# A decoder layer's causal mask: from a TensorE accumulation to GpSimd selects on the exponentials

## The chip, the cores and the metric

The kernel runs on one core of a Trainium2 chip. The metric is the device time of one execution in microseconds. It is float32 work with some bfloat16 matmuls, about 86,000 instructions in one launch.

## The reference

64 sequences of 256 tokens with 256 channels go through self-attention, cross-attention and a routed feed-forward net, each on a layer-normalized input and each added to the residual. The change touches the self-attention only (16 heads of 16 channels):

```python
att = jnp.einsum('bhtd,bhsd->bhts', q, k) / math.sqrt(D)
causal = jnp.tril(jnp.ones((T, T), dtype=bool))
att = jnp.where(causal, att, -jnp.inf)
att = jax.nn.softmax(att, axis=-1)
y = jnp.einsum('bhts,bhsd->bhtd', att, v)
```

Then follow the cross-attention, over 120 context rows with one key found per context row by an argmax, and the feed-forward net (256 to 1024 to 256, one of four experts for each token).

## The kernel before

The first three quarters of the run are a loop over the 64 sequences (`steps`), and the last quarter is a loop over 35 tiles of 512 tokens for the feed-forward net. Five engines run five programs of their own, each a fixed order written out by hand. They meet only in semaphores. The loop is a pipeline: iteration i projects sequence i, attends within sequence i-1, does the first half of the cross-attention of i-2, the second half of i-3 and the routing of i-4. One iteration takes about 49 us.

Queries and keys are split in bfloat16 parts, written to DRAM and read back in packed form (SyncE's queue: `store_parts`, `pack`). `cq_parts` to `parts_qc` to `QC` is that round trip for the cross-attention.

The self-attention computes the scores twice. The first pass (`self_for_max`, row by query) gives each query's maximum, and has a causal mask of its own, `mask_s`. The second pass (`self_scores`, row by key, steps n = 0 to 11) includes the negative maximum in the product. Three steps make a group g of four heads: two steps of two heads each for the first 128 keys against all 256 queries, and one step of four heads for the last 128 keys against the last 128 queries. Each step ends with one more matmul, L647, that adds `mask_t` (-1e30 above the diagonal) through an identity matrix onto the 128x128 blocks on the diagonal: 256 columns in the first two steps of a group, 512 columns in the third. ScalarE then takes the exponential (`self_exp`, L964) into `PA` (first 128 keys) or `PB` (last 128 keys), and `self_values` (L660 for PA, L662 for PB) multiplies with the values. `self_values` of group g waits until exponential 3g+3 is done.

The order on TensorE in the last part of an iteration: scores 0, 1, 2, a small ranking product, score 3; then `cross_for_max` 0 (L724), which needs `QC` from DRAM; then scores and cross products in turn (score 4, cross 1, score 5, cross 2, values of group 0, score 6, cross 3, and so on up to score 11), values of group 1 after cross 5, values of group 2 after score 11, values of group 3, a small transpose, and `turn_y` (L559), which transposes the attention's result. Score n waits for exponential n-2, since there are two PSUM banks for scores. VectorE takes the maxima of the cross products (`cross_max`, L1131), and after the sixth it takes the statistics of the next sequence (`ln1_statistics`, L1092 and L1096).

GpSimd's order in an iteration: `q_parts` and `k_parts` (L1528, L1531), `cq_parts` (L1535), the reciprocal root for the third layer norm, the root for the next sequence's first layer norm (`root`, L1480 and L1483), two indirect DMAs of routed rows (`send_rows`), the root for the second layer norm, and nine small steps that split the context keys (`split_k`). Each engine executes its queue strictly in order.

Of the kernel before, what the change touches and what calls it, by code (L numbers as in the profile page):

```python
# [8 lines left out]
BF16 = mybir.dt.bfloat16  # L9
# [5 lines left out]
P = 128  # L15
C = 256
KC = C // P
T = 256
# [48 lines left out]
def decoder_kernel(nc, x, ctxT, wqkvT, bqkT, bv, wqT, wkvT, wcT, w_router, w1, b1T, wo, bo, gamma, beta, consts, out):  # L67
# [3 lines left out]
    with ExitStack() as stack:  # L71
        def sb(name, shape, dt=F32):
            return stack.enter_context(nc.sbuf_tensor(name, shape, dt))

        def signal(name, per_sequence, step=1):
            return Signal(stack.enter_context(nc.semaphore(name)), per_sequence * step)
# [8 lines left out]
        psum = stack.enter_context(nc.psum_tensor("psum", [P, 8, 512], F32))  # L85
# [12 lines left out]
        ident_bf = sb("ident_bf", [P, P], BF16)  # L98
        ones_bf = sb("ones_bf", [P, P], BF16)
        mask_s = sb("mask_s", [P, P], BF16)  # L100
        mask_t = sb("mask_t", [P, P], BF16)
        consts_sb = sb("consts_sb", [P, TILE_NOS + B * T // TILE + E - 1])
        iota_m = consts_sb[:, 3 * P:3 * P + M]
        part_mask = consts_sb[:, 3 * P + M:3 * P + M + 3]
# [32 lines left out]
        def during_attention(name, shape, dt=F32):  # L137
            return attention_stack.enter_context(nc.sbuf_tensor(name, shape, dt))
# [14 lines left out]
        QP = during_attention("QP", [P, 2, H, T], BF16)  # L153
        KP = during_attention("KP", [P, 2, H, T], BF16)
# [4 lines left out]
        PA = during_attention("PA", [P, H, T])  # L159
        PB = during_attention("PB", [P, H, P])  # L160
# [124 lines left out]
        place_step = signal("place_step", 5)  # L285
        consts_in = semaphore("consts_in")
        consts_ready = semaphore("consts_ready")
        VECTOR_CONSTS = 9
        gpsimd_consts = semaphore("gpsimd_consts")
        GPSIMD_CONSTS = 7  # L290
        N_FIRST_LOADS = 3
# [22 lines left out]
        st_made = signal("st_made", 12)  # L314
# [18 lines left out]
        q_mid = signal("q_mid", 1)  # L333
        k_mid = signal("k_mid", 1)
        exp_done = signal("exp_done", 12)
        mxT_copied = signal("mxT_copied", 1)
        yT_copied = signal("yT_copied", 2)
        czT_copied = signal("czT_copied", 1)
# [41 lines left out]
        passed_pool = semaphore("passed_pool")  # L380
# [14 lines left out]
        def runs(i, lag):  # L395

            return not isinstance(i, int) or 0 <= i - lag < B
# [151 lines left out]
        def _(pe):  # L549
            def latest(*readers):  # L550


                for sig, b, k in readers:
                    if not isinstance(b, int) or 0 <= b < B:
                        return sig.sem, sig.value(b, k)
                return consts_ready, VECTOR_CONSTS

# [65 lines left out]
            def self_scores(i, par, n):  # L623

                b, q = i - 1, 1 - par
                KS = KR + 2
                g, r = divmod(n, 3)
                bank = ST_BANKS[n % 2]
                if n == 0:
                    pe.wait_ge(mx_packed[q].sem, mx_packed[q].value(b // 2))  # L630
                elif n == 1:
                    pe.wait_ge(*latest((cyC_copied, i - 3, 1), (exp_done, i - 2, 12)))
                else:
                    pe.wait_ge(exp_done.sem, exp_done.value(b, n - 1))
                if r < 2:
                    for j in range(2):
                        h = 4 * g + 2 * r + j
                        pe.matmul(psum[:, bank, j * T:(j + 1) * T], KP[0:KS, q, h, 0:P], QP[0:KS, q, h, :], start=(j == 0), stop=False, skip_group_check=True)  # L638
                    diagonal = psum[:, bank, :].rearrange("p (j k) -> p j k", j=2)[:, :, 0:P]
                    masks = 2  # L640
                else:
                    for j in range(4):
                        h = 4 * g + j
                        pe.matmul(psum[:, bank, j * P:(j + 1) * P], KP[0:KS, q, h, P:T], QP[0:KS, q, h, P:T], start=(j == 0), stop=False, skip_group_check=True)  # L644
                    diagonal = psum[:, bank, :]
                    masks = 4
                pe.matmul(diagonal, ident_bf[:], mask_t[:].unsqueeze(1).broadcast_to([P, masks, P]), start=False, stop=True, skip_group_check=True).then_inc(st_made.sem, 1)  # L647

            def self_values(i, par, g):

                b, q = i - 1, 1 - par
                bank, col = Y_BANKS[g // 2], (g % 2) * T
                if g == 0:
                    pe.wait_ge(v_copied.sem, v_copied.value(b))
                    pe.wait_ge(*latest((match_step, i - 2, 2 * NT), (q_rest_made, i, 1)))
                elif g == 2:
                    pe.wait_ge(*latest((kmask_made, i - 2, 1), (k_rest_made, i, 1)))
                pe.wait_ge(exp_done.sem, exp_done.value(b, 3 * g + 3))
                for j in range(4):
                    pe.matmul(psum[32 * j:32 * j + 32, bank, col:col + T], V[:, q, 0, 4 * g + j, :], PA[:, 4 * g + j, :], start=True, stop=False, skip_group_check=True)  # L660
                for j in range(4):
                    last = pe.matmul(psum[32 * j:32 * j + 32, bank, col + P:col + T], V[:, q, 1, 4 * g + j, :], PB[:, 4 * g + j, :], start=False, stop=True, skip_group_check=True)  # L662
                if g % 2 == 1:
                    last.then_inc(pv_made.sem, 1)
# [176 lines left out]

            pe.wait_ge(consts_ready, VECTOR_CONSTS)
            pe.wait_ge(first_weights_in, 16 * N_FIRST_LOADS)
# [226 lines left out]
        def _(dve):  # L1070
            made = [0]

            def constant(ins):
                ins.then_inc(consts_ready, 1)
                made[0] += 1
# [1 line left out]
            dve.wait_ge(consts_in, 16)  # L1077
            constant(dve.tensor_copy(ident_bf[:], consts_sb[:, 0:P]))
            constant(dve.tensor_copy(mask_s[:], consts_sb[:, P:2 * P]))
            constant(dve.tensor_copy(mask_t[:], consts_sb[:, 2 * P:3 * P]))  # L1080
            constant(dve.memset(ones_bf[:], 1.0))
            constant(dve.tensor_copy(before_bf[:], consts_sb[:, BEFORE:BEFORE + P]))
            constant(dve.tensor_copy(next_row[:], consts_sb[:, NEXT_ROW:NEXT_ROW + E]))
# [2 lines left out]
            constant(dve.memset(minus_half[:], -0.5))  # L1086
            assert made[0] == VECTOR_CONSTS

# [234 lines left out]

            dve.wait_ge(consts_ready, VECTOR_CONSTS)
            ln1_statistics(0, 0)
# [149 lines left out]
        def _(pool):  # L1475
            def root(b, step, mean_var, rs, made, eps, NT=NT):

                pool.wait_ge(step.sem, step.value(b, 2 * NT))
                pool.sem_inc(passed_pool, 1)
                pool.tensor_scalar(rs[:], mean_var[:, :, 1], eps, None, ALU.add).then_inc(made.sem, 1)  # L1480
                pool.wait_ge(made.sem, made.value(b, 1))
                pool.sem_inc(passed_pool, 1)
                pool.tensor_tensor(rs[:], rs[:], minus_half[:, 0:NT], ALU.pow).then_inc(made.sem, 1)  # L1483

            def send_rows(i, par):

                b = i - 4
                pool.wait_ge(place_step.sem, place_step.value(b))
                pool.sem_inc(passed_pool, 1)
                pool.wait_ge(x2_made.sem, x2_made.value(b))  # L1490
                pool.sem_inc(passed_pool, 1)
                pool.wait_ge(number_made.sem, number_made.value(b))
                pool.sem_inc(passed_pool, 1)
                for t in range(NT):
                    pool.indirect_dma_start(out=rows_dram, out_offset=bass.IndirectOffsetOnAxis(ap=row_u[:, par, t:t + 1], axis=0),
                                            in_=x2[:, par, t, :], in_offset=None).then_inc(rows_sent[par].sem, 16)
# [27 lines left out]
            def body(i, par):  # L1524
                if runs(i, 0):
                    pool.wait_ge(q_mid.sem, q_mid.value(i))
                    pool.sem_inc(passed_pool, 1)
                    pool.tensor_tensor(q_parts[:, 2, :], q_rest[:], q_parts[:, 1, :], ALU.subtract).then_inc(q_low.sem, 1)  # L1528
                    pool.wait_ge(k_mid.sem, k_mid.value(i))
                    pool.sem_inc(passed_pool, 1)  # L1530
                    pool.tensor_tensor(k_parts[:, 2, :], k_rest[:], k_parts[:, 1, :], ALU.subtract).then_inc(k_low.sem, 1)  # L1531
                if runs(i, 2):
                    pool.wait_ge(cq_mid.sem, cq_mid.value(i - 2))
                    pool.sem_inc(passed_pool, 1)
                    pool.tensor_tensor(cq_parts[:, 2, :], cq_rest[:], cq_parts[:, 1, :], ALU.subtract).then_inc(cq_low.sem, 1)  # L1535
                if runs(i, 3):
                    root(i - 3, ln3_step, rmv, rrstd, ln3_rstd, LN_EPS)
                if runs(i, 0):
                    root(i + 1, ln1_step, mv, rstd, ln1_rstd, LN_EPS)
                if runs(i, 4):  # L1540
                    send_rows(i, par)
                if runs(i, 1):
                    root(i - 1, ln2_step, cmv, crstd, ln2_rstd, LN_EPS)
                    split_k(i, par)

            pool.wait_ge(consts_ready, VECTOR_CONSTS)
            root(0, ln1_step, mv, rstd, ln1_rstd, LN_EPS)
# [136 lines left out]
```

## Time and profile before

| | |
|---|---|
| median of 3 runs | 4378.67 us (4378.36 to 4382.7) |
| profiled execution, span | 4384.2 us |
| TensorE busy | 3487.1 us, 80% |
| VectorE busy | 3030.9 us, 69% |
| ScalarE busy | 1595.7 us, 36% |
| GpSimd busy | 1468.2 us, 33% |
| granted TensorE clock, mean | 0.870 of full |
| loop over sequences | to about 3240 us |

The span runs from the first to the last instruction of the profiled execution; no time of that execution outside its span is given, so the span is compared with the median of the timed runs directly. Busy time is the share of an engine's instructions that are executing, and a high share doesn't show that the engine sets the end.

### The profile page before, as it was taken

What the parts mean: (1) busy time and instruction counts of PE and PEld (TensorE: products, weight loads), DVE (VectorE), ACT (ScalarE), POOL (GpSimd) and SP (SyncE); (2) the same over time, 40 slices, a digit from 0 to 9 for tenths busy, and PEclk for the clock granted to TensorE, in tenths of its full rate; (3) what the DMA queues carried; (4) which work ended last, traced back from release to release, by engine and by line L of the source; (5) the groups of instructions that cost most, each with busy time, mean ns of one, the idle gap of its engine ahead of it and who ended that gap; (6) DMA issues with size and microseconds to landing.
All of it is one profiled execution on the core that took longest, in us unless ns stands there. A gap on an engine that the chain in (4) does not pass through costs nothing.

```text
span 4384.2 us, 86021 instructions
## 1 busy us (share of the span) xinstructions
PE 3487.1 (80%) x26632; PEld 2620.2 (60%) x26632; DVE 3030.9 (69%) x7302; ACT 1595.7 (36%) x2976; POOL 1468.2 (33%) x1785
## 2 busy tenths in 40 slices
PE   5788778887788777887788778887748888888887
PEld 3555555555555555555555555555537777777777
DVE  3666656665666656665666656665649999999997
ACT  2444444444444444444444444444412222222221
POOL 3222222222222222222222222222225656565655
PEclk7888888888888888888888889888858889888888
DMA  6455554455455554555455554555321212212120
GB/s 126 78 92 94 96 89 84 89 99 93 85 90 95 94 89 84 93 96 95 82 90 95 94 89 89 92 95 93 61 76 63 68 65 67 67 64 67 65 67 32
DMA packets 341784, 366.25 MB, mean 84 GB/s; under 512 B 58456, under 2 KB 319071, under 8 KB 341728
## 3 DMA queue, kind: packets, MB, share of 16 engines
q1 hardware_dynamic: 324768, 330.85, 41.8%
q0 software_dynamic: 12864, 33.64, 2.1%
q10 hardware_dynamic: 4096, 1.06, 0.1%
q8 instruction: 30, 0.49, 0.1%
q14 instruction: 26, 0.21, 0.0%
HBM read 251.56 MB, written 113.32 MB: 83 GB/s over the span
## 4 chain that ended last, share of the span: by engine, by line
PE 29%; DVE 24%; DMA 21%; issue 12%; ACT 4%; POOL 4%; SPq 3%; DVEq 1%; POOLq 0%; ACTq 0%
DMA parts_qc<-cq_parts 12%; DMA QC<-parts_qc 8%; DVE hT_high L1405 8%; PE psum L660 4%; PE psum L724 4%; SPq L457 3%; PE psum L565 3%; PE psum L638 3%; PE psum L647 2%; PE psum L611 2%; PE psum L559 2%; PE psum L751 2%; POOL cq_parts L1535 2%; PE psum L662 2%; PE psum L644 2%
## 5 line engine op out<-in xcount | busy, mean ns | idle before, releaser
L1131 DVE TENSOR_REDUCE cnegmax<-psum 128x4 f32<-128x480 f32 x512 | 324.3, 654 | 662.1 <-PE psum L724 661.9
L964 ACT ACTIVATE PA<-psum 128x512 f32<-128x512 f32 x512 | 294.9, 596 | 881.3 <-PE psum L647 879.9
L724 PE MATMUL psum<-KCx,QC 97*128 97x120 bf16 x2048 | 243.7, 256 | 332.7 <-DMA QC<-parts_qc 331.0
L1058 ACT ACTIVATE hT<-psum,b_sb 128x512 f32<-128x512 f32 x280 | 193.2, 690 | 848.1 <-PE psum L884 848.1
L900 PE MATMUL psum<-wo_high,hT_low 128*128 128x256 f32 x1120 | 385.4, 344 | 131.1 <-DVE hT_low L1408 69.0
L1124 DVE TENSOR_REDUCE negmax<-psum 128x2 f32<-128x512 f32 x512 | 340.9, 687 | 154.1 <-PE psum L614 153.8
L724 PEld LDWEIGHTS psum<-KCx,QC 97*128 97x128 bf16 x2048 | 190.4, 119 | 404.3 <-issue 347.3
L638 PE MATMUL psum<-QP,KP 98*128 98x256 bf16 x1024 | 240.8, 327 | 164.7 <-DMA QP<-mxT 164.7
L1405 DVE CAST hT_high<-hT 128x512 fp32r<-128x512 f32 x280 | 359.7, 1295 | 3.9 <-ACT hT L1058 3.7
L900 PEld LDWEIGHTS psum<-wo_high,hT_low 128*128 128x128 f32 x1120 | 252.7, 226 | 177.1 <-DVE hT_low L1408 95.9
L900 PE MATMUL psum<-wo_low,hT_high 128*128 128x256 f32 x1120 | 354.9, 317 | 0.0
L900 PE MATMUL psum<-wo_high,hT_high 128*128 128x256 f32 x1120 | 352.7, 315 | 0.0
L1480 POOL TENSOR_SCALAR rstd<-mv 128x2 f32<-128x2 f32 x65 | 15.2, 234 | 991.4 <-DVE mv L1096 991.4
L976 ACT ACTIVATE PC<-psum 120x512 f32<-120x512 f32 x512 | 291.3, 594 | 86.2 <-PE psum L740 80.2
L647 PE MATMUL psum<-mask_t,ident_bf 128*128 128x256 bf16 (+1 forms) x768 | 292.5, 381 | 0.0
L565 PE MATMUL psum<-zT,wqkv_sb 128*128 128x256 f32 x1024 | 241.0, 389 | 23.6 <-ACT zT L917 23.6
L900 PEld LDWEIGHTS psum<-wo_low,hT_high 128*128 128x128 f32 x1120 | 256.2, 229 | 0.0
L900 PEld LDWEIGHTS psum<-wo_high,hT_high 128*128 128x128 f32 x1120 | 254.1, 227 | 0.0
L614 PE MATMUL psum<-mask_s,ident_bf 128*128 128x256 bf16 (+1 forms) x768 | 240.3, 313 | 0.0
L565 PEld LDWEIGHTS psum<-zT,wqkv_sb 128*128 128x128 f32 x1024 | 191.6, 192 | 62.8 <-issue 32.5
L884 PE MATMUL psum<-fzT_high,w_low 128*128 128x512 f32 x560 | 219.4, 392 | 7.6 <-DVE fzT_low L1400 7.6
L1535 POOL TENSOR_TENSOR cq_parts<-cq_rest,cq_parts 128x512 bf16<-128x512 f32 x64 | 74.0, 1156 | 444.9 <-ACT cq_parts L917 444.9
(211 smaller groups left out, 8867.8 us busy)
## 6 DMA issues: line engine op xcount, KB each, us to landing
QP<-parts_q SPq DMA_DIRECT2D x384, 128.0 KB, 4.5
KP<-parts_k SPq DMA_DIRECT2D x384, 128.0 KB, 7.8
QC<-parts_qc SPq DMA_DIRECT2D x384, 128.0 KB, 4.6
w_sb<-in_w SPq DMA_DIRECT2D x35, 1024.0 KB, 4.8
parts_q<-q_parts SPq DMA_DIRECT2D x64, 384.0 KB, 2.6
parts_k<-k_parts SPq DMA_DIRECT2D x64, 384.0 KB, 2.6
parts_qc<-cq_parts SPq DMA_DIRECT2D x64, 384.0 KB, 8.4
fx<-rows_dram SPq DMA_DIRECT2D x35, 514.0 KB, 3.8
```

What stands on the lines that cost most here:

```text
L565: last = pe.matmul(psum[:, bank, m * width:(m + 1) * width], lhs(kc, m), rhs(kc), start=(kc == 0), stop=(kc == KC - 1))
L614: pe.matmul(diagonal, ident_bf[:], mask_s[:].unsqueeze(1).broadcast_to([P, masks, P]), start=False, stop=True, skip_group_check=True).then ...
L638: pe.matmul(psum[:, bank, j * T:(j + 1) * T], KP[0:KS, q, h, 0:P], QP[0:KS, q, h, :], start=(j == 0), stop=False, skip_group_check=True)
L647: pe.matmul(diagonal, ident_bf[:], mask_t[:].unsqueeze(1).broadcast_to([P, masks, P]), start=False, stop=True, skip_group_check=True).then ...
L724: last = pe.matmul(psum[:, bank, j * M:(j + 1) * M], QC[0:KS, par, 4 * g + j, t * P:(t + 1) * P], KCx[0:KS, par, 0:M], start=True, stop=True)
L884: last = pe.matmul(psum[:, bank, :], lhs, rhs, start=(n == 0), stop=(n == len(products) - 1))
L900: last = pe.matmul(psum[:, 4 + half, j * C:(j + 1) * C], lhs, rhs, start=(m == 0 and n == 0), stop=(m == MI - 1 and n == 2))
L964: act.activation(dst, psum[:, ST_BANKS[n % 2], :], ACT.Exp, scale=D ** -0.5).then_inc(exp_done.sem, 1)
L976: act.activation(PC[0:M, 2 * n:2 * n + 2, :].rearrange("p h n -> p (h n)"), psum[0:M, ST_BANKS[n % 2], :], ACT.Exp, scale=D ** -0.5).then_ ...
L1124: dve.tensor_reduce(negmax[:, 1, h:h + 2], bank.rearrange("p (h k) -> p h k", h=2), AX_X, ALU.max).then_inc(max_done.sem, 1)
L1131: dve.tensor_reduce(cnegmax[:, t, 4 * g:4 * g + 4], psum[:, S_BANKS[n % 2], 0:4 * M].rearrange("p (h k) -> p h k", h=4), AX_X, ALU.max).th ...
L1405: dve.tensor_copy(hT_high[:, m, :], hT[:, m, :]).then_inc(h_high_made.sem, 1)
```

## The change

The mask matmul of the second score pass goes away, with the constant `mask_t`, and the last score matmul of a step signals `st_made` in its place. GpSimd, for each group of four heads, waits for the group's third exponential and then runs two affine selects in place: one on the first 128 columns of `PA` of the four heads, one on `PB` of the four heads, each 128 partitions by 4 x 128 float32. Weights of keys later than the query become 0. `self_values` waits for the second of these selects, not for the exponential. On GpSimd, groups 0 to 2 stand after the root of the third layer norm and before the root of the next sequence's first layer norm; group 3 stands after that root and before `send_rows`. The first pass keeps its `mask_s`.

```diff
-                pe.matmul(diagonal, ident_bf[:], mask_t[:].unsqueeze(1).broadcast_to([P, masks, P]), start=False, stop=True, skip_group_check=True).then_inc(st_made.sem, 1)
+                last.then_inc(st_made.sem, 1)
...
-                pe.wait_ge(exp_done.sem, exp_done.value(b, 3 * g + 3))
+                pe.wait_ge(causal.sem, causal.value(b, 2 * g + 2))
...
-            constant(dve.tensor_copy(mask_t[:], consts_sb[:, 2 * P:3 * P]))
...
+            def drop_later_keys(b, g):
+
+                heads = slice(4 * g, 4 * g + 4)
+                pool.wait_ge(exp_done.sem, exp_done.value(b, 3 * g + 3))
+                pool.sem_inc(passed_pool, 1)
+                pool.affine_select(out=PA[:, heads, 0:P], in_=PA[:, heads, 0:P], pattern=[[0, 4], [1, P]], base=0, channel_multiplier=-1,
+                                   compare_op=ALU.is_ge, fill=0.0).then_inc(causal.sem, 1)
+                pool.affine_select(out=PB[:, heads, :], in_=PB[:, heads, :], pattern=[[0, 4], [1, P]], base=0, channel_multiplier=-1,
+                                   compare_op=ALU.is_ge, fill=0.0).then_inc(causal.sem, 1)
...
                 if runs(i, 3):
                     root(i - 3, ln3_step, rmv, rrstd, ln3_rstd, LN_EPS)
+                if runs(i, 1):
+                    for g in range(3):
+                        drop_later_keys(i - 1, g)
                 if runs(i, 0):
                     root(i + 1, ln1_step, mv, rstd, ln1_rstd, LN_EPS)
+                if runs(i, 1):
+                    drop_later_keys(i - 1, 3)
                 if runs(i, 4):
                     send_rows(i, par)
```

## Rows read from the trace of the kernel before

**Rows 1.** The first page: its span, and busy time of each engine.

```profile
span 4384.2 us, 86021 instructions
...
PE 3487.1 (80%) x26632; PEld 2620.2 (60%) x26632; DVE 3030.9 (69%) x7302; ACT 1595.7 (36%) x2976; POOL 1468.2 (33%) x1785
```

**Rows 2.** The page: the chain that ended last, by engine, then by line.

```profile
PE 29%; DVE 24%; DMA 21%; issue 12%; ACT 4%; POOL 4%; SPq 3%; DVEq 1%; POOLq 0%; ACTq 0%
DMA parts_qc<-cq_parts 12%; DMA QC<-parts_qc 8%; DVE hT_high L1405 8%; PE psum L660 4%; PE psum L724 4%; SPq L457 3%; PE psum L565 3%; PE psum L638 3%; PE psum L647 2%; PE psum L611 2%; PE psum L559 2%; PE psum L751 2%; POOL cq_parts L1535 
```

**Rows 3.** Waits from 400 to 3100 us: waiter, releaser: us in total, times, longest.

```profile
PE psum L724 <- DMA QC<-parts_qc: 291.0, 55, 6.2
```

**Rows 4.** TensorE in order of time: start us, us, engine, line, out<-in [idle before].

```profile
1886.52 0.56 PE L724 MATMUL psum<-KCx,QC 97*128 97x120 bf16 x4 [5.87 <-DMA QC<-parts_qc]
...
1887.29 0.42 PE L647 MATMUL psum<-mask_t,ident_bf 128*128 128x256 bf16 x1
1887.51 0.61 PE L724 MATMUL psum<-KCx,QC 97*128 97x120 bf16 x4
...
1891.11 0.27 PE L647 MATMUL psum<-mask_t,ident_bf 128*128 128x256 bf16 x1
1891.22 0.37 PE L724 MATMUL psum<-KCx,QC 97*128 97x120 bf16 x4
...
1892.83 0.64 PE L660 MATMUL psum<-PA,V 128*32 128x256 f32 x8
...
1895.05 0.38 PE L647 MATMUL psum<-mask_t,ident_bf 128*128 128x512 bf16 x1
1895.36 0.64 PE L660 MATMUL psum<-PA,V 128*32 128x256 f32 x8
...
1896.12 0.64 PE L660 MATMUL psum<-PA,V 128*32 128x256 f32 x8
...
1897.69 1.09 PE L559 MATMUL psum<-consts_sb,yT 128*128 128x128 f32 x8 [0.42 <-ACT yT L917]
```

**Rows 5.** The page's costliest groups: line, engine, operation | busy, mean ns | idle before.

```profile
L647 PE MATMUL psum<-mask_t,ident_bf 128*128 128x256 bf16 (+1 forms) x768 | 292.5, 381 | 0.0
```

**Rows 6.** GpSimd groups by shape over the whole run.

```profile
L1528 POOL TENSOR_TENSOR q_parts<-q_rest,q_parts 128x512 bf16<-128x512 f32 x64 | 73.8, 1153 | 12.2 <-ACT q_parts L917 9.5
...
L1510 POOL TENSOR_SCALAR kc_b<-kc_m,consts_sb 96x120 f32<-96x120 bf16 x64 | 37.1, 580 | 13.3 <-POOL kc_a L1509 13.3
...
L1549 POOL MEMSET V<- 128x2048 f32 x1 | 1.8, 1797 | 0.0
```

**Rows 7.** GpSimd in order of time, in the same iteration.

```profile
1895.54 0.24 POOL L1480 TENSOR_SCALAR rstd<-mv 128x2 f32<-128x2 f32 x1 [15.11 <-DVE mv L1096]
1895.96 0.71 POOL L1483 TENSOR_TENSOR rstd<-rstd,minus_half 128x2 f32<-128x2 f32 x1 [0.18 <-POOL rstd L1480]
```

**Rows 8.** ScalarE in order of time: the last exponentials of groups 0 to 3.

```profile
1880.23 0.60 ACT L964 ACTIVATE PB<-psum 128x512 f32<-128x512 f32 x1 [0.22 <-PE psum L647]
...
1889.01 0.60 ACT L964 ACTIVATE PB<-psum 128x512 f32<-128x512 f32 x1 [0.66 <-PE psum L647]
...
1892.73 0.60 ACT L964 ACTIVATE PB<-psum 128x512 f32<-128x512 f32 x1 [0.16 <-PE psum L647]
...
1895.46 0.60 ACT L964 ACTIVATE PB<-psum 128x512 f32<-128x512 f32 x1 [0.16 <-PE psum L647]
```

**Rows 9.** VectorE in order of time, in the same iteration.

```profile
1894.92 0.42 DVE L1096 BATCH_NORM_AGGREGATE mv<-stats 128x2 f32<-128x6 f32 x2
```

**Rows 10.** Busy us by engine in stretches; PEclk, DMA share, GB/s stand last.

```profile
1876.30:1880.80 4.50, 2.02 (x21) 1.16 (x19) 2.48 (x10) 1.65 (x4) 0.94 (x2) 1.00 0.58 138
...
1886.50:1891.10 4.60, 4.58 (x38) 3.03 (x39) 2.57 (x5) 1.19 (x2) 0.00 (x0) 0.50 0.00 0
...
1896.70:1900.00 3.30, 2.54 (x31) 1.87 (x20) 2.39 (x10) 1.60 (x4) 2.19 (x2) 1.00 0.14 45
```

**Rows 11.** The same view for a stretch of the iteration before.

```profile
1836.90:1843.30 6.40, 6.32 (x51) 4.49 (x52) 3.37 (x8) 1.99 (x4) 0.00 (x0) 0.50 0.00 0
```

More of the change, by code:

```diff
@@ L100, in decoder_kernel @@
         mask_s = sb("mask_s", [P, P], BF16)
-        mask_t = sb("mask_t", [P, P], BF16)
         consts_sb = sb("consts_sb", [P, TILE_NOS + B * T // TILE + E - 1])
@@ L287, in decoder_kernel @@
         consts_ready = semaphore("consts_ready")
-        VECTOR_CONSTS = 9
+        VECTOR_CONSTS = 8
         gpsimd_consts = semaphore("gpsimd_consts")
@@ L335, in decoder_kernel @@
         exp_done = signal("exp_done", 12)
+        causal = signal("causal", 8)
         mxT_copied = signal("mxT_copied", 1)
@@ L637, in self_scores @@
                         h = 4 * g + 2 * r + j
-                        pe.matmul(psum[:, bank, j * T:(j + 1) * T], KP[0:KS, q, h, 0:P], QP[0:KS, q, h, :], start=(j == 0), stop=False, skip_group_check=True)
-                    diagonal = psum[:, bank, :].rearrange("p (j k) -> p j k", j=2)[:, :, 0:P]
-                    masks = 2
+                        last = pe.matmul(psum[:, bank, j * T:(j + 1) * T], KP[0:KS, q, h, 0:P], QP[0:KS, q, h, :], start=(j == 0), stop=(j == 1), skip_group_check=True)
                 else:
@@ L643, in self_scores @@
                         h = 4 * g + j
-                        pe.matmul(psum[:, bank, j * P:(j + 1) * P], KP[0:KS, q, h, P:T], QP[0:KS, q, h, P:T], start=(j == 0), stop=False, skip_group_check=True)
-                    diagonal = psum[:, bank, :]
-                    masks = 4
-                pe.matmul(diagonal, ident_bf[:], mask_t[:].unsqueeze(1).broadcast_to([P, masks, P]), start=False, stop=True, skip_group_check=True).then_inc(st_made.sem, 1)
+                        last = pe.matmul(psum[:, bank, j * P:(j + 1) * P], KP[0:KS, q, h, P:T], QP[0:KS, q, h, P:T], start=(j == 0), stop=(j == 3), skip_group_check=True)
+                last.then_inc(st_made.sem, 1)
             def self_values(i, par, g):
```

## The prediction

> **What bounds the kernel now.** I read the first page, then the chain, the waits, and one iteration engine by engine. The page shows TensorE at 80% and GpSimd at 33% busy [rows 1], which invites the thought that work should go from the one to the other. The chain corrects it: TensorE is only 29% of the chain that ended last, VectorE 24%, and DMA 21%, most of it the round trip of `cq_parts` through DRAM [rows 2]. The waits say where that trip is felt: TensorE stands before cross product 0 for 291.0 us in 55 iterations, 5.3 us in each [rows 3]. So an iteration is a loop of three parts: a head (from `turn_y` to `cq_parts`), the round trip, and a tail that starts when `QC` has landed and ends with the values of group 3. What TensorE does before cross product 0 is hidden behind the round trip. What it does in the tail is not.
>
> The tail of the iteration that I follow runs from 1886.52 to `turn_y` at 1897.69 [rows 4]. Values of group 1 start at 1892.83, of group 2 at 1895.36, of group 3 at 1896.12, and `turn_y` comes 1.57 us after the last. The next head's first steps wait for that.
>
> **What the change removes.** 768 mask matmuls, 292.5 us busy [rows 5]. Of the twelve in an iteration, four (scores 0 to 3) stand ahead of the wait for `QC` and are worth nothing. The cover is the 5.87 us idle before cross product 0 [rows 4]; they are under 1 us. Eight stand in the tail. What one costs is the distance to the next start, since matmuls overlap: 0.22 us (1887.29 to 1887.51) for 256 columns at the half clock, 0.11 us (1891.11 to 1891.22) at the full one [rows 4], and I count twice that for 512 columns. Scores 4 and 5 run at the half clock (0.22 + 0.43), scores 6 to 11 at the full one (4 x 0.11 + 2 x 0.22): 1.53 us in a tail, if TensorE sets its pace. The dropped copy of `mask_t` on VectorE is one instruction in the setup, hidden behind the first loads, and under 1 us even if it weren't.
>
> **What it adds.** Eight affine selects of 128 x 512 float32 in each iteration, 512 in all. No such instruction is in the trace, so their time S is bounded. The shortest GpSimd work of this kind is a memset, 1797 ns for 2048 elements, so 0.45 us for 512. The nearest in shape is a tensor-tensor of 128x512, 1153 ns [rows 6]. The most expensive slope is that of a tensor-scalar, 580 ns for 120 elements [rows 6] against 0.24 us for 2 [rows 7]: 2.9 ns an element, 0.24 + 510 x 0.0029 = 1.73 us. I take 1.15 us, the row of the same shape, as an estimate: a select reads one operand and not two, but computes an index and a comparison as well. The range keeps 0.45 and 1.73.
>
> The Trainium skill (GPSIMD Engine Reference, section 7) gives 2.03 cycles an element for a body that compares and selects, and half that when unrolled; at its 1.2 GHz that would be 0.87 or 0.44 us for 512 elements. By the first, an S of some 1.0 us with a fixed part, the sum below would be about 4 x 0.15 = 0.6 us an iteration smaller. No row here shows a select. The same page (section 4.1) advises against elementwise work on this engine; that speaks against the change only where GpSimd's time is seen, so the question is where.
>
> **Where the selects stand on the path.** Group 0: its last exponential ends at 1880.83 [rows 8], and GpSimd has been idle since 15.11 us before 1895.54, that is since 1880.43 [rows 7]. Its two selects (2.3 us) end near 1883.3, before `QC` lands at 1886.5: hidden. If the cover were gone, they would cost 2.3 us.
>
> Group 1: the last exponential ends at 1889.61 now [rows 8], about 0.65 us sooner without the masks of scores 4 and 5: 1888.96. GpSimd reacts after about 0.2 us (VectorE's `mv` ends at 1895.34 [rows 9], the root starts at 1895.54 [rows 7]). Selects from 1889.15 to 1891.45. The values of group 1 would come at 1892.83 - 1.09 = 1891.74 (five masks less): just hidden, up to S = 1.25.
>
> Group 2: the exponential ends at 1893.33, less 1.09 is 1892.24; selects 1892.45 to 1894.75. The values of group 2 would come at about 1894.05: a wait of 0.8 us.
>
> Group 3: its select is queued behind the root of the next sequence's first layer norm, and this root is behind group 2's selects. The root needs `mv`, which ends at 1895.34 [rows 9], about 1.1 us sooner now, so it starts when the selects of group 2 let it, 1894.75. It takes 1.13 us (1895.54 to 1896.67 [rows 7]): until 1895.9. The last exponential ends at 1896.06 - 1.53 = 1894.53, long before. Two selects until 1898.2, values of group 3 at 1898.3, where they were at 1896.12 [rows 4]. **The first term is +2.2 us an iteration**, the saved 1.53 us already in it. Written out, the values of group 3 start at the latest of three times: 1893.68 + 4S (group 2's exponential, four selects, the root, 0.1 to TensorE), 1890.37 + 6S (six selects from group 1 on), and 1895.68 + 2S (the root alone ahead, `mv` at 1894.25). At 1.15 the first decides.
>
> Nothing takes that delay up. The ScalarE copy, `turn_y`, the residual and the next head hang on these values, the round trip hangs on the head, and the next iteration waits for `QC` again. The next exponentials wait for the same values (`pv_made`), but come much later. Behind group 3's selects on GpSimd stand `send_rows`, the second layer norm's root and the split of context keys; the root's input comes later by the same delay, and the two indirect DMAs in front of it end before it is due. SyncE's queue gets nothing new. Busy time of GpSimd grows by 512 x 1.15 = 590 us, which by itself costs nothing.
>
> **The clock.** Between the start of group 2's values and that of group 3's, TensorE would now be busy for 0.76 us in some 3.5 to 4.2 us. The stretch before 1880.80 had 2.02 us busy in 4.5, and the clock was granted at half (1.2 GHz) from there on; the one from 1896.70 to 1900.00 had 2.54 in 3.3 and kept full (2.4 GHz) [rows 10]. The new stretch looks like the first. Once low, the clock stayed so for 4.6 us of nearly unbroken work in this tail [rows 10] and 6.4 us in the one before [rows 11]. Such a stretch loses half of itself, 2.3 to 3.2 us, of work that would fall on `turn_y`, the turns and the projections at the head's start. I take 2.6 us as the **second term**; a part could hide behind VectorE's residual and layer norm, and if the clock were low in the whole tail it would be more.
>
> The Trainium skill (TensorE: Matmul & The Clock Gate, section "Why this matters for your kernels") warns of idle gaps between bursts of matmuls that are longer than the gap of some 2.7 us expected here; by it the clock would hold. The trace doesn't bear that out: its stretch of 4.5 us with 2.02 us of work was followed by the half clock. So I follow the trace, and keep the other outcome as the second rival.
>
> **The sum.** 2.2 + 2.6 = 4.8 us in each of the 62 iterations that have all parts (the first and last have less): +298 us. Against the span of 4384.2 that is 4682. The span lies 5.5 us above the median of the timed runs, 4378.67, so the forecast is 4677, said as 4680.
>
> **The rivals.**
> Slower selects. At S = 1.73 the first two times above are 1900.60 and 1900.75, so +4.6, with the clock +7.2 an iteration: +446, 4825. If S were twice the tensor-tensor's, 2.3, six selects decide: 1904.2, +8.1 + 2.6, 4384 + 663, about 5040. For it: the tensor-scalar's slope. Against it: one operand. 15%.
> The clock holds. +2.2 x 62 = +136: 4515. For it: a stretch with 2.54 us of work in 3.3 kept the clock [rows 10], and the new one is the emptier only if both waits come. The Trainium skill's rule on gaps (above) speaks for it too. Against it: the drop in [rows 10]. 15%.
> Short selects. At S = 0.45 the third time decides, 1896.58: +0.46; with the clock's 2.6 +190 (4569), without +29 (4408). 11%.
> Faster. The root is no longer in front: if the statistics come early enough for the root to end before group 3's exponential, the values of group 3 start at 1894.53 + 0.2 + 2S + 0.1. With S = 0.45 that is 1895.73, 0.4 us sooner than before, -25 us: 4355. It decides below S = 0.65, and only with the root gone. As the queue is, the third time above asks for S under 0.22. Against it: the memset's row, and `mv`, whose input is cross maximum 5. 3%.
> No measurable change: S near 0.6 in that same case. 2%.
>
> **How the numbers follow.** The forecast, with S from 0.8 to 1.5 and a lower clock, has 54%; its own range is 2.6 + (1.3 to 3.6) in an iteration, so 4620 to 4765. The range for all reaches down to short selects with a held clock and up past the tensor-scalar's price: 4420 to 4860, which leaves out some 2 in 10, at the top mostly. About 0.2% (9 us) is what a measurement of this kernel can tell from no change. Faster 3%, same 2%, slower 95%.
>
> **What the profile after would show.** The group of the select, with its mean: the largest unknown. L647 gone, TensorE's busy time down by some 290 us minus what a lower clock adds. A wait of L660 for GpSimd's PB, two in an iteration, the longer one 2 to 3 us, none for groups 0 and 1. The root at L1483 directly before group 3's selects. Granted clock falling between 1 and 4 us before group 3's values, and the mean clock under 0.870. The idle time before L724 about as before, since both ends of the round trip shift together; if it shrinks instead, the delay was taken up there, and the prediction is wrong. It is wrong too if selects are under 0.5 us or above 2 us.

## The result, and the profile after

The changed kernel takes 4494.98 us (median of 4 runs, 4487.36 to 4499.14), the kernel before 4378.51 us beside it. The ratio is 1.0253, 95% interval 1.0234 to 1.0271: 2.5% slower, some 111 us, or 1.79 us in each of 62 iterations. The forecast was slower by 6.9%. Its range held the time, its number did not come near.

The first page after: the span, the busy times, and two of the costliest groups, the select on PA and the product of the values.

```profile
span 4497.4 us, 85514 instructions
...
PE 3451.9 (77%) x25864; PEld 2604.6 (58%) x25864; DVE 3081.7 (69%) x7301; ACT 1582.6 (35%) x2976; POOL 1771.7 (39%) x2297
...
L1485 POOL TENSOR_SCALAR_AFFINE_SELECT PA<-PA 128x512 f32<-128x512 f32 x256 | 162.5, 635 | 654.5 <-ACT PB L960 654.0
...
L656 PE MATMUL psum<-PA,V 128*32 128x256 f32 x2048 | 207.2, 484 | 123.4 <-POOL PB L1487 123.4
```

GpSimd's selects take 635 ns each, not 1.15 us. L656 (L660 before) now has idle time in front of it, 123.4 us, all of it ended by GpSimd's second select; the rows of L660 before have none [rows 4]. GpSimd's busy time grew by 303.5 us, and TensorE's fell by only 35 us though 292.5 us of mask matmuls are gone [rows 5].

One tail on TensorE after (start us, us), to set beside [rows 4]: cross product 0, the values of groups 1, 2 and 3, `turn_y`, and the next projections.

```profile
1902.28 0.56 PE L720 MATMUL psum<-KCx,QC 97*128 97x120 bf16 x4 [6.37 <-DMA QC<-parts_qc]
...
1907.64 0.64 PE L656 MATMUL psum<-PA,V 128*32 128x256 f32 x8
...
1909.84 0.64 PE L656 MATMUL psum<-PA,V 128*32 128x256 f32 x8
...
1912.71 0.89 PE L656 MATMUL psum<-PA,V 128*32 128x256 f32 x8 [2.01 <-POOL PB L1487]
...
1914.72 1.87 PE L559 MATMUL psum<-consts_sb,yT 128*128 128x128 f32 x8 [0.52 <-ACT yT L913]
...
1917.80 3.72 PE L565 MATMUL psum<-zT,wqkv_sb 128*128 128x256 f32 x16 [0.33 <-ACT zT L913]
```

ScalarE's last exponentials of groups 1 to 3 in that tail, to set beside [rows 8]:

```profile
1904.13 0.60 ACT L960 ACTIVATE PB<-psum 128x512 f32<-128x512 f32 x1 [0.23 <-PE psum L642]
...
1907.48 0.60 ACT L960 ACTIVATE PB<-psum 128x512 f32<-128x512 f32 x1
...
1909.94 0.60 ACT L960 ACTIVATE PB<-psum 128x512 f32<-128x512 f32 x1
```

VectorE's statistics for the next sequence, to set beside [rows 9]:

```profile
1909.71 0.42 DVE L1091 BATCH_NORM_AGGREGATE mv<-stats 128x2 f32<-128x6 f32 x2
```

And GpSimd's queue in that tail, to set beside [rows 7]: two selects for group 1, two for group 2, the root of the next layer norm, two for group 3.

```profile
1904.89 0.63 POOL L1485 TENSOR_SCALAR_AFFINE_SELECT PA<-PA 128x512 f32<-128x512 f32 x1 [7.43 <-ACT PB L960]
1905.47 0.63 POOL L1487 TENSOR_SCALAR_AFFINE_SELECT PB<-PB 128x512 f32<-128x512 f32 x1
1908.24 0.64 POOL L1485 TENSOR_SCALAR_AFFINE_SELECT PA<-PA 128x512 f32<-128x512 f32 x1 [2.13 <-ACT PB L960]
1908.83 0.63 POOL L1487 TENSOR_SCALAR_AFFINE_SELECT PB<-PB 128x512 f32<-128x512 f32 x1
1910.33 0.23 POOL L1475 TENSOR_SCALAR rstd<-mv 128x2 f32<-128x2 f32 x1 [0.86 <-DVE mv L1091]
1910.75 0.71 POOL L1478 TENSOR_TENSOR rstd<-rstd,minus_half 128x2 f32<-128x2 f32 x1 [0.18 <-POOL rstd L1475]
1911.43 0.63 POOL L1485 TENSOR_SCALAR_AFFINE_SELECT PA<-PA 128x512 f32<-128x512 f32 x1
1912.02 0.63 POOL L1487 TENSOR_SCALAR_AFFINE_SELECT PB<-PB 128x512 f32<-128x512 f32 x1
```

Group 1 starts its selects at 1904.89 and has them at 1906.1; its values start at 1907.64, so they don't wait. Group 2 starts at 1908.24 and has them at 1909.46; its values start at 1909.84 and don't wait either. Group 3's last exponential ends at 1910.54, but GpSimd is in the root from 1910.33 to 1911.46. The root waited 0.86 us for VectorE's statistics, which end at 1910.13. The selects end at 1912.65 and the values of group 3 start at 1912.71, after 2.01 us without work. That is 10.43 us after cross product 0, where it was 9.60 [rows 4].

The rest comes behind it. `turn_y` lasts 1.87 us for 1.09 [rows 4]. The busy time in two stretches shows why (TensorE first, the granted clock third from the end):

```profile
1908.40:1912.00 3.60, 2.30 (x36) 1.32 (x32) 3.46 (x10) 2.17 (x4) 2.55 (x5) 1.00 0.00 0
1912.00:1915.50 3.50, 2.27 (x22) 1.64 (x23) 1.15 (x3) 0.85 (x2) 2.73 (x4) 0.64 0.10 38
```

TensorE was busy for 2.30 us of 3.60 and then ran at 0.64 of the full clock in the next stretch, a mixture of the half and the full level. Shorter stretches part the two:

```profile
1913.00:1916.30 3.30, 2.78 (x26) 2.23 (x19) 0.54 (x3) 0.85 (x2) 1.91 (x2) 0.50 0.23 82
1916.40:1920.00 3.60, 3.27 (x20) 2.81 (x19) 2.56 (x9) 1.15 (x3) 0.48 (x2) 1.00 0.50 157
```

The clock stands at half while `turn_y` runs and is full again before the projections. It doesn't fall in every iteration: `turn_y` takes more than 1.3 us in 55 of the 64 iterations after and in none before. In the iterations after that keep 1.09 us, the two distances behind the values of group 3 are those of the kernel before (1.57 and 2.27 us on the mean, against 1.58 and 2.29).

VectorE's busy time grew too, by 51 us [rows 1]. Two operations that run beside group 3's selects have some 45 us of it. The two before, then after:

```profile
1896.73 0.19 DVE L1111 SCALAR_TENSOR_TENSOR cmx<-cnegmax,cmx 128x32 bf16<-128x32 f32 x1
1896.85 0.73 DVE L1102 TENSOR_SCALAR z<-x_in,mv,rstd 128x256 f32<-128x256 f32 x2
...
1911.53 0.58 DVE L1106 SCALAR_TENSOR_TENSOR cmx<-cnegmax,cmx 128x32 bf16<-128x32 f32 x1
1912.03 1.12 DVE L1097 TENSOR_SCALAR z<-x_in,mv,rstd 128x256 f32<-128x256 f32 x2
```

They end at 1912.11 and 1913.15, and TensorE turns their results after the values of group 3 and after `turn_y`. So this isn't on the path here.

For a whole view I read the same five starts of TensorE in 54 or 55 iterations of every trace and averaged the distances between them. The last column is the period. The kernels of the experiments, described below, stand in it already.

```
us, mean over iterations      cross 0 to       values 3    turn_y to     projections   period
                              values of 3      to turn_y   projections   to cross 0
before                          9.75            1.58         2.29          35.66       49.28
after                          10.59            1.96         3.16          35.37       51.07
masks removed, no select        8.61            1.58         2.29          35.95       48.43
selects added, masks kept      11.21            1.70         2.48          35.79       51.18
group 3 before the root        10.14            1.58         2.56          35.66       49.94
busy wait                      10.79            1.58         2.29          35.88       50.53
group 3 by mask                 8.94            1.58         2.29          35.69       48.50
two more in group 3            12.01            2.01         3.44          35.18       52.64
two more in group 1            10.70            1.78         3.26          35.16       50.89
```

The difference of the periods, 51.07 - 49.28 = 1.79 us, times 62 is 111 us, the whole result. It has three parts: +0.84 up to the values of group 3, +0.38 + 0.87 = +1.25 from there to the projections, and -0.29 in the rest.

### The profile page after: what moved, and what is told of

The parts are those of the page before. It is cut to its first block, busy times and chain, and to the rows that moved or that the text cites. A ratio compares the mean times of both kernels' runs of the same rounds, so it can differ in the third digit from the quotient of the medians.

```text
span 4497.4 us, 85514 instructions
## 1 busy us (share of the span) xinstructions
PE 3451.9 (77%) x25864; PEld 2604.6 (58%) x25864; DVE 3081.7 (69%) x7301; ACT 1582.6 (35%) x2976; POOL 1771.7 (39%) x2297
## 4 chain that ended last, share of the span: by engine, by line
PE 30%; DVE 22%; DMA 20%; issue 13%; ACT 6%; POOL 5%; SPq 3%; DVEq 1%; POOLq 0%; ACTq 0%
DMA parts_qc<-cq_parts 11%; DMA QC<-parts_qc 8%; DVE hT_high L1400 8%; PE psum L565 7%; PE psum L559 4%; SPq L457 3%; PE psum L656 3%; PE psum L720 2%; PE psum L611 2%; PE psum L747 2%; PE psum L896 2%; POOL cq_parts L1540 2%; PE psum L614 1%; ACT PC L972 1%; PE psum L736 1%
## 5 line engine op out<-in xcount | busy, mean ns | idle before, releaser
L720 PEld LDWEIGHTS psum<-KCx,QC 97*128 97x128 bf16 x2048 | 178.0, 120 | 440.4 <-issue 364.2
L1485 POOL TENSOR_SCALAR_AFFINE_SELECT PA<-PA 128x512 f32<-128x512 f32 x256 | 162.5, 635 | 654.5 <-ACT PB L960 654.0
L638 PE MATMUL psum<-QP,KP 98*128 98x256 bf16 x1024 | 226.2, 320 | 144.1 <-DMA QP<-mxT 143.8
L656 PE MATMUL psum<-PA,V 128*32 128x256 f32 x2048 | 207.2, 484 | 123.4 <-POOL PB L1487 123.4
L1475 POOL TENSOR_SCALAR rrstd<-rmv 128x2 f32<-128x2 f32 x64 | 14.2, 222 | 610.1 <-DVE rmv L1091 610.1
```

Source lines behind the costliest of these rows:

```text
L638: last = pe.matmul(psum[:, bank, j * T:(j + 1) * T], KP[0:KS, q, h, 0:P], QP[0:KS, q, h, :], start=(j == 0), stop=(j == 1), skip_group_che ...
L720: last = pe.matmul(psum[:, bank, j * M:(j + 1) * M], QC[0:KS, par, 4 * g + j, t * P:(t + 1) * P], KCx[0:KS, par, 0:M], start=True, stop=True)
```

## The experiments

All were timed beside the kernel before on the same chip. The ratios are to the kernel before and are to be read beside 1.0253 for the change; a ratio times 4378.5 us puts a time on the scale of the expectations.

**1. The removal alone.** The changed kernel without its selects, so keys later than the query keep their weight in the diagonal blocks.

```diff
-                pe.wait_ge(causal.sem, causal.value(b, 2 * g + 2))
+                pe.wait_ge(exp_done.sem, exp_done.value(b, 3 * g + 3))
...
-                    for g in range(3):
-                        drop_later_keys(i - 1, g)
...
-                    drop_later_keys(i - 1, 3)
```

> The mask matmuls of the second score pass are gone and nothing takes their place, so later keys keep their weight within the diagonal blocks. In the changed kernel the values of group 2 start 7.56 us after cross product 0, before it was 8.84, so theory A (TensorE sets the pace of the tail) expects the values of group 3 to start 1.3 to 1.5 us sooner than before in each of 62 iterations: 4379 - 80 to 95, so 4285 to 4300. Rival B (the exponentials or the maxima set the pace of the tail) expects under 0.3 us an iteration, so 4360 to 4380.

Measured: 4320.72 us, ratio 0.9844 (0.9827 to 0.9861), that is -68 us, or 4310 us where 4285 to 4300 was expected. The values of group 3 come 9.75 - 8.61 = 1.14 us sooner, a little under the 1.3 expected. In the table 0.29 us of it is lost between the projections and cross product 0, but the execution in the trace was the slowest of the five (4336.23 us, 15.5 us over the median, 0.25 us an iteration), so that loss may be of this execution alone. Theory A holds in kind: TensorE sets the pace of the tail, and the masks there are worth 1.14 us and not the 1.53 of their summed distances.

**2. The addition alone.** The masks stay, the selects are added as in the change.

```diff
                 pe.matmul(diagonal, ident_bf[:], mask_t[:]...).then_inc(st_made.sem, 1)
...
-                pe.wait_ge(exp_done.sem, exp_done.value(b, 3 * g + 3))
+                pe.wait_ge(causal.sem, causal.value(b, 2 * g + 2))
...
+                    for g in range(3):
+                        drop_later_keys(i - 1, g)
...
+                    drop_later_keys(i - 1, 3)
```

> The mask matmuls stay and the eight selects are added as in the change. Theory A (group 3's selects behind the root, plus a clock that falls in the gap): values of group 3 come at root end + 2 selects = 1.9 us later than before, and the gap of 1.9 us without work lets the clock fall for about 1 us more: 4379 + 62 x 2.9 = 4559. Rival C (the clock costs nothing, only the queue): 4379 + 62 x 1.9 = 4497. Rival D (the selects are hidden and the added time has its cause in the removal): 4379.

Measured: 4510.84 us, ratio 1.0282 (1.0259 to 1.0305). The queue costs 1.46 us, not 1.9, the head between the values and the projections 0.31 us, the rest 0.13. TensorE in one of its tails, cross product 0 and the values of groups 2 and 3:

```profile
1858.15 0.56 PE L725 MATMUL psum<-KCx,QC 97*128 97x120 bf16 x4 [5.21 <-DMA QC<-parts_qc]
...
1866.72 0.64 PE L661 MATMUL psum<-PA,V 128*32 128x256 f32 x8
...
1869.27 0.64 PE L661 MATMUL psum<-PA,V 128*32 128x256 f32 x8 [1.69 <-POOL PB L1493]
```

The wait of 1.69 us stands here too. The time came out near rival C's number and well below theory A's 2.9 us an iteration, because both terms were smaller: `turn_y` is slow in only 16 of 64 iterations of this kernel. What matters more: 1.0282 with the masks and 1.0253 without. Once group 3 waits for GpSimd, taking the masks out is worth some 0.3%, and the two intervals overlap; alone it was worth 1.6%.

**3. Group 3's selects before the root.**

```diff
-                    for g in range(3):
+                    for g in range(4):
                         drop_later_keys(i - 1, g)
                 if runs(i, 0):
                     root(i + 1, ln1_step, mv, rstd, ln1_rstd, LN_EPS)
-                if runs(i, 1):
-                    drop_later_keys(i - 1, 3)
```

> The changed kernel with one move: group 3's selects stand before the root of the next sequence's first layer norm on GpSimd. The last exponential ends at 1910.54 in the changed kernel's iteration, so the selects can end at 1911.94 and the values of group 3 start at 1912.04, not 1912.71. Theory A: -0.67 us from the queue, and TensorE's gap of 2.0 us shrinks to 1.35 us, which may keep the clock: 4495 - 41 = 4454 if the clock still falls, down to 4495 - 103 = 4392 if it holds. Rival E (the root was late itself and its delay now hits the next layer norm): no gain, 4490 to 4500.

Measured: 4429.61 us, ratio 1.009 (1.0075 to 1.0104), that is some 70 us of the 111 back. One of its tails, cross product 0, the values of groups 2 and 3, and `turn_y`:

```profile
1867.31 0.56 PE L720 MATMUL psum<-KCx,QC 97*128 97x120 bf16 x4 [5.96 <-DMA QC<-parts_qc]
...
1875.48 0.64 PE L656 MATMUL psum<-PA,V 128*32 128x256 f32 x8
...
1877.63 0.64 PE L656 MATMUL psum<-PA,V 128*32 128x256 f32 x8 [1.29 <-POOL PB L1487]
...
1879.20 1.42 PE L559 MATMUL psum<-consts_sb,yT 128*128 128x128 f32 x8 [0.63 <-ACT yT L913]
```

The values of group 3 start 10.32 us after cross product 0 (10.14 on the mean, 0.45 sooner than in the change) and the wait is 1.29 us. `turn_y` takes 1.42 us here, so the clock still falls in some iterations, 19 of 64, but what the head has over the kernel before shrinks from 1.25 to 0.27 us on the mean. In the other iterations nothing of it is left (1.58 and 2.29 us), so the 0.27 is the clock's too and not the later root's. The queue's order was the cause of most of the loss. Rival E, which expected no gain, is out. What stays of the queue is 10.14 - 9.75 = 0.39 us: two selects behind the last exponential cost more than the masks in the tail saved, even with no root between.

**4. A busy wait.** Eight matmuls nobody reads between the values of groups 2 and 3.

```diff
                 if runs(i, 1):
+                    if runs(i, 3):
+                        for _ in range(8):
+                            pe.matmul(psum[:, 6, :], ident_bf[:], mask_s[:].unsqueeze(1).broadcast_to([P, 4, P]), start=True, stop=True)
                     self_values(i, par, 3)
```

> The changed kernel with eight extra matmuls of 512 columns between the values of groups 2 and 3, into a PSUM bank that is free then; their result is read by nobody. They take 1.7 us at the full clock, in a gap of 2.0 us. Theory A (the gap lets the clock fall, which costs about 1 us an iteration after the 0.8 us of the queue): the granted clock stays full over turn_y and the time falls to 4495 - 62 x 1.0 = 4433. Rival C (what is over the 0.8 us doesn't come from the clock): 4490 to 4500, or more if the extra work delays the values of group 3.

Measured: 4464.11 us, ratio 1.0171 (1.0154 to 1.0189). More work on TensorE made the kernel faster. One tail (cross product 0, the eight, the values of group 3, `turn_y`) and the busy time of two stretches:

```profile
1884.08 0.56 PE L720 MATMUL psum<-KCx,QC 97*128 97x120 bf16 x4 [6.06 <-DMA QC<-parts_qc]
...
1893.30 1.90 PE L834 MATMUL psum<-mask_s,ident_bf 128*128 128x512 bf16 x8
1895.13 0.64 PE L656 MATMUL psum<-PA,V 128*32 128x256 f32 x8
...
1896.70 1.09 PE L559 MATMUL psum<-consts_sb,yT 128*128 128x128 f32 x8 [0.63 <-ACT yT L916]
```

```profile
1893.30:1896.70 3.40, 2.78 (x30) 1.28 (x26) 1.87 (x5) 1.05 (x3) 2.92 (x5) 1.00 0.03 12
1896.70:1900.00 3.30, 2.97 (x21) 2.64 (x22) 2.50 (x8) 1.32 (x3) 0.60 (x1) 1.00 0.23 75
```

The clock stays at 1.00, `turn_y` is back at 1.09 us, and the two columns behind the values of group 3 are those of the kernel before to the hundredth, 1.58 and 2.29. `turn_y` is slow in 2 of 64 iterations. VectorE's two slowed operations are slow here as in the change (`z` takes 0.598 us on the mean in both, 0.432 before), so they aren't the cause. The whole +1.25 us is the clock's, and comes from the gap. The gain in time was smaller, 0.54 us an iteration for 1.0 expected: the values of group 3 came 0.20 us later, and the last part took 35.88 and not 35.37 us. Rival C, by which the clock has no part in it, is out; the last part is taken up below.

**5. Group 3 by mask.** Groups 0 to 2 by selects, group 3 as before the change.

```diff
-                last.then_inc(st_made.sem, 1)
+                if g == 3:
+                    last = pe.matmul(diagonal, ident_bf[:], mask_t[:].unsqueeze(1).broadcast_to([P, masks, P]), start=False, stop=True, skip_group_check=True)
+                last.then_inc(st_made.sem, 1)
...
-                pe.wait_ge(causal.sem, causal.value(b, 2 * g + 2))
+                if g < 3:
+                    pe.wait_ge(causal.sem, causal.value(b, 2 * g + 2))
+                else:
+                    pe.wait_ge(exp_done.sem, exp_done.value(b, 12))
...
-                if runs(i, 1):
-                    drop_later_keys(i - 1, 3)
```

> Groups 0 to 2 by selects as in the change, group 3 by the mask matmuls as before. Theory A (the cost is group 3's selects behind the root, the gain is the masks that leave the tail): with all masks gone the values of group 3 start 8.61 us after cross product 0; group 3's three masks give back 0.44: 9.05, where before has 9.75, and no gap for the clock to fall in. -0.7 us, or -0.4 where the transfer of cq_parts takes 0.3 us longer as it did in the run without masks: 4335 to 4355 on the scale where before is 4379, faster than both. Rival F (the selects of groups 1 and 2 cost something too, by waits or by sharing with VectorE): 4379 or slower.

Measured: 4336.86 us, ratio 0.9894 (0.9875 to 0.9912): 1.1% faster than the kernel before. Of the kernels here that mask all scores it is the fastest. One tail, cross product 0, the values of groups 2 and 3, `turn_y`:

```profile
1860.20 0.56 PE L730 MATMUL psum<-KCx,QC 97*128 97x120 bf16 x4 [5.36 <-DMA QC<-parts_qc]
...
1867.99 0.64 PE L666 MATMUL psum<-PA,V 128*32 128x256 f32 x8
...
1868.75 0.64 PE L666 MATMUL psum<-PA,V 128*32 128x256 f32 x8
...
1870.33 1.09 PE L560 MATMUL psum<-consts_sb,yT 128*128 128x128 f32 x8 [0.26 <-ACT yT L923]
```

The values of group 3 follow those of group 2 in 0.76 us, with no wait, 8.55 us after cross product 0 (8.94 on the mean, 9.05 expected). Six selects an iteration lie fully beside other work, and VectorE's busy time is 3027.3 us, no more than before [rows 1]. Rival F is out.

**6 and 7. Two more selects, in group 3 and in group 1.** They read constants and write a spare tile.

```diff
+                if g == 3:          # g == 1 in experiment 7
+                    if begun(b - 1):
+                        pool.wait_ge(spare_made.sem, spare_made.value(b - 1))
+                        pool.sem_inc(passed_pool, 1)
+                    for k in range(2):
+                        pool.affine_select(out=spare[:, k], in_=consts_sb[:, 0:4 * P].rearrange("p (h k) -> p h k", h=4), pattern=[[0, 4], [1, P]], base=0, channel_multiplier=-1,
+                                           compare_op=ALU.is_ge, fill=0.0).then_inc(spare_made.sem, 1)
```

> The changed kernel with two more selects of the same shape ahead of group 3's own; they read constants and write a spare tile. Each select adds 0.61 us to GpSimd's queue. Theory A: values of group 3 come 1.2 to 1.4 us later, and a longer gap lets the clock fall in all iterations: 62 x 1.3 = 81 us, and up to 62 x 2 if the low clock lasts longer; 4575 to 4620 beside 4495. Rival G (group 3 is not limited by GpSimd's queue): under 20 us.

Measured: 4600.55 us, ratio 1.0492 (1.0471 to 1.0512). The values of group 3 come 12.01 - 10.59 = 1.42 us later, and `turn_y` is slow in all 64 iterations. One tail, cross product 0 and the values of group 3:

```profile
1854.87 0.56 PE L722 MATMUL psum<-KCx,QC 97*128 97x120 bf16 x4 [5.97 <-DMA QC<-parts_qc]
...
1866.88 0.64 PE L658 MATMUL psum<-PA,V 128*32 128x256 f32 x8 [2.73 <-POOL PB L1496]
```

> The same two extra selects ahead of group 1's own. Group 1's exponential ends about 2.45 us after cross product 0; with 0.2, four selects (2.44) and 0.1 its values could start at 5.2, where they start at 5.52 now, and GpSimd is free at 5.1, before group 2's exponential ends at 5.8. Theory A: hidden, 4490 to 4505. Rival F (busy GpSimd time costs wherever it stands): as much as the same two in group 3, 4575 or more.

Measured: 4485.73 us, ratio 1.0237 (1.0218 to 1.0256), no more than the change itself. Cross product 0 and the values of groups 1 and 3 in one of its tails:

```profile
1847.51 0.56 PE L722 MATMUL psum<-KCx,QC 97*128 97x120 bf16 x4 [5.26 <-DMA QC<-parts_qc]
...
1852.97 0.64 PE L658 MATMUL psum<-PA,V 128*32 128x256 f32 x8
...
1858.21 0.97 PE L658 MATMUL psum<-PA,V 128*32 128x256 f32 x8 [2.12 <-POOL PB L1496]
```

Group 1's values start with no wait behind four selects, 5.46 us after cross product 0 (in the change 5.36). The same work costs 2.4% behind the root (1.0492 against 1.0253) and nothing 6.7 us earlier in the same queue (the two extra selects start 2.79 us after cross product 0 here and 9.45 us after it in experiment 6). GpSimd's busy time as such costs nothing, and rivals F and G are out.

## Why the prediction was wrong, point by point

**What bounds the kernel: right.** The masks in the tail, and they alone, had a price (experiment 1), and cover for group 0 held: no wait of its values in the trace after.

**The size of S: wrong, and the first step that failed.** It decides the first term, 2.2 us forecast and 0.84 measured. I took 1.15 us, the tensor-tensor's row. The select took 0.635 us, and 0.59 us from start to start: 1.22 us for the pair (1911.43 to 1912.65). It lies near the memset's bound of 0.45 us and far from the tensor-scalar's 1.73. The Trainium skill (GPSIMD Engine Reference, section 7) had 2.03 cycles an element for a compare-and-select body and half that unrolled, by my estimate from it 0.87 and 0.44 us; the measurement lies between, and each of the two was nearer to it than the two-operand row.

**The queue's step: right, with the smaller S.** Of the three times that I wrote down, the third decides at this S: 1895.68 + 2 x 0.61 = 1896.90, +0.78 us. Measured +0.84 on the mean. Experiment 3 shows the root in front (-0.45 us when it goes behind), experiment 6 the slope of the queue. The wait of 0.8 us for group 2's values did not happen; by my sum it hangs on S = 1.15. Two numbers around this step were off and moved no forecast: without the masks those values would start at 1895.36 - 1.53 = 1893.83 and not 1894.05, and S = 0.8 gives +1.2 us by the third time and not +1.3.

**The masks' worth: near.** 1.53 us by distances, 1.14 measured. It changes nothing in this sum, for in the third time only VectorE's statistics, some 1.1 us sooner in my sum, carry it. Measured, they end 7.85 us after cross product 0 (1910.13), where they ended 8.82 us after it [rows 4, 9]: 0.97 us sooner.

**The clock: right in kind, wrong in size.** It fell, with a gap of 2.0 us and 2.30 us of work in 3.6. But the low stretch was short. I took its length from the low phases after the wait for `QC`, 4.6 and 6.4 us of unbroken work; this one had ended before the projections, which take 3.72 us from 1917.80 as they did before, and covered only group 3's values, the small transpose and `turn_y`. It cost 1.25 us on the mean over all iterations, those in which the clock held included, and not 2.6. My rival "the clock holds" was wrong: the Trainium skill (TensorE: Matmul & The Clock Gate, section "Why this matters for your kernels") warns only of longer gaps than this one, and here the trace doesn't agree, since a gap of 2.0 us with sparse work before it was enough.

**Nothing takes the delay up: wrong by 0.29 us.** From the projections to cross product 0 the time fell from 35.66 to 35.37 us. My sign for this, a shorter idle time before cross product 0, missed it: that wait grew, from 291.0 us in 55 iterations to 315.0 us in 53. It grew also where only masks were taken out (experiment 1: 332.8 us in 56) and not where they stayed (experiment 2: 286.4 us in 53), so it comes from the four masks ahead of it. The distances say where the 0.29 us lies. On the mean the packs of the keys are issued 15.40 us after the projections before and 15.17 after: they don't hang on the projections alone, so part of a late projection is taken up there. From them to the packs of `QC` it is 12.09 us in both, though the store of `cq_parts` between them, issued 18.87 and 18.96 us after the projections, doesn't move with the packs. SyncE's queue after, the last packs of the keys, the store, and the packs that wait for it:

```profile
1881.83 2.67 SPq L457 DMA_DIRECT2D KP<-parts_k  x6
1885.39 0.38 SPq L447 DMA_DIRECT2D parts_qc<-cq_parts  x1
1893.78 2.67 SPq L457 DMA_DIRECT2D QC<-parts_qc  x6
```

The same three in experiment 6:

```profile
1886.83 2.67 SPq L459 DMA_DIRECT2D KP<-parts_k  x6
1890.95 0.38 SPq L449 DMA_DIRECT2D parts_qc<-cq_parts  x1
1898.69 2.67 SPq L459 DMA_DIRECT2D QC<-parts_qc  x6
```

From the store's issue to the next packs it is 8.39 us in the one and 7.74 in the other; from the keys' packs 11.95 and 11.86. So the later the store comes behind the packs, the shorter it lasts: they appear to share one end. On the mean it lands some 0.7 us after the last of the keys' packs in every one of the nine traces. But no run here moved the packs alone, so it stays an argument, and what lets the packs come sooner after late projections was not followed.

**The sum.** By my steps with measured sizes: +0.84 + 1.25 - 0.29 = +1.80 us, 62 x 1.80 = 112 us. With mine: 2.2 + 2.6 = 4.8. Short selects with the clock's fall was the third rival with 11%, at 4569 for S = 0.45; the measured case is that rival, with half the clock's price. Both terms erred to the same side, so nothing cancelled: the time lies below the forecast's own range of 4620 to 4765, and only the wide range, which reached down to short selects and a held clock, has it.

## What to carry to other kernels

Work taken from a busy engine is worth only what it puts on the path, and the engine that gets it must be looked at by its queue, not by its busy share: the same two selects cost 2.4% behind one root and nothing in front of another group. When a step of a pipeline moves to another engine, leave the last one where it was; here three groups by select and the last by mask is 1.1% faster than before, all four by select 2.5% slower. And count a new wait on TensorE twice, once for itself and once for the clock that it may cost to the work behind it.

## What the runs showed of the hardware

An affine select of 128 x 512 float32 on GpSimd takes 0.635 us, 0.59 us from start to start, against 1.153 us for a tensor-tensor of that shape [rows 6]. Eight useless matmuls in a gap of 2 us made a kernel 0.8% faster (1.0253 to 1.0171), because the clock stayed at its full level. TensorE's granted clock stood at 0.50 from 1913.0 to 1916.3, after a gap of 2.0 us, and at 1.00 from 1916.4; in the work after the long wait for the transfer it stood at 0.50 for 4.6 and 6.4 us [rows 10, 11]. The same gap let it fall in 55 of 64 iterations, one of 1.3 us in 19 of 64 (experiment 3).

Beside group 3's selects two VectorE operations took longer than in the kernel before: a tensor-scalar of 128 x 256 float32 0.598 us for 0.432, and a scalar-tensor-tensor of 128 x 32 float32 0.566 us for 0.193. Groups 0 to 2's selects slowed neither (experiment 5: 0.433 and, by VectorE's busy time, nothing else).
